# The sixteen remainders x_lo subtracted by GpSimd in VectorE's place

## What is computed

```
def _L0_cond_ref(x, thresholds, deltas, zero_points):       # G = 8 groups by |x|
    gi = jnp.sum(jnp.abs(x)[..., None] <= thresholds, axis=-1)
    idx = jnp.minimum(gi, G - 1)
    d = deltas[idx]; zp = zero_points[idx]
    x_quant = jnp.clip(jnp.round(x / d) + zp, 0, N_LEVELS - 1)
    return jnp.where(gi == G, jnp.float32(0), (x_quant - zp) * d)
...
x = x + _L0_ffn_ref(_L0_cond_ref(x, ...), router_w, A, B)    # top 2 of 4 low-rank experts
x = x + _L1_ffn_ref(_L1_cond_ref(x, itok, W, lora_A, lora_B_w), gate, kernel, bias, ...)
```

## Time and profile before

| | us |
|---|---|
| median of 3 runs | 467.94 (467.78 to 469.76) |
| profiled execution | 467.9 |
| its span | 466.1 |
| TensorE busy | 459.5 (99%) |
| VectorE busy | 389.0 (83%) |
| ScalarE busy | 356.8 (77%) |
| GpSimd busy | 5.4 (1%) |

### The profile page before, as it was taken

One profiled execution on the slowest core, in us unless ns is written; L12 is line 12 of the kernel. 1 busy time (PEld: TensorE's weight loads), 2 busy tenths in 40 slices (PEclk: granted clock), 3 DMA queues, 4 the chain that ended last, 5 costly groups with the idle time before them and its releaser, 6 DMA issues.

```text
span 466.1 us, 5628 instructions
## 1 busy us (share of the span) xinstructions
PE 459.5 (99%) x2182; PEld 353.3 (76%) x2182; DVE 389.0 (83%) x381; ACT 356.8 (77%) x299; POOL 5.4 (1%) x11
## 2 busy tenths in 40 slices
PE   8999999999999999999999999999999999999996
PEld 8537888888688887778777877787787778767874
DVE  1376989998999979999999999799899997999300
ACT  1499979893799799598599987995999797895001
POOL 0000000000000000000000000000000000000000
PEclk9999999999999999999999999999999999999999
DMA  8998324301244333505125107105214013011102
GB/s 273 363 368 334 99 57 148 101 12 51 61 127 167 92 49 101 191 1 157 43 104 157 58 1 234 69 4 158 91 56 159 0 56 136 28 30 45 46 1 90
DMA packets 35836, 50.35 MB, mean 108 GB/s; under 512 B 26626, under 2 KB 26882, under 8 KB 33538
## 3 DMA queue, kind: packets, MB, share of 16 engines
q1 hardware_dynamic: 34802, 42.66, 28.3%
q0 software_dynamic: 1008, 7.34, 4.2%
HBM read 39.51 MB, written 10.49 MB: 107 GB/s over the span
## 4 chain that ended last, share of the span: by engine, by line
PE 87%; ACT 4%; DMA 3%; DVE 2%; issue 2%; SPq 1%; ACTq 0%
PE bank L984 13%; PE bank L986 13%; PE bank L985 13%; PE bank L961 6%; PE bank L893 6%; PE bank L867 5%; PE bank L915 5%; PE bank L936 5%; PE bank L932 5%; PE bank L933 5%; DMA kst<-k_in 3%; PE bank L824 3%; PE bank L889 2%; PE bank L982 2%; ACT level L415 1%
## 5 line engine op out<-in xcount | busy, mean ns | idle before, releaser
L636 DVE COPY_PREDICATED val<-inside,val 128x2048 f32<-128x2048 uint8 x56 | 142.3, 2542 | 0.3
L426 ACT ACTIVATE val<-level,shift,small 128x2048 f32<-128x2048 int16 x64 | 133.9, 2091 | 2.3 <-PE bank L867 1.9
L415 ACT ACTIVATE level<-xq,inv 128x2048 int16<-128x2048 f32 x64 | 127.9, 1998 | 0.9
L984 PE MATMUL bank<-p_hi,x_hi 128*128 128x512 f32 x256 | 101.9, 398 | 0.0
L986 PE MATMUL bank<-p_hi,x_lo 128*128 128x512 f32 x256 | 100.1, 391 | 0.0
L985 PE MATMUL bank<-p_lo,x_hi 128*128 128x512 f32 x256 | 99.9, 390 | 0.0
L618 DVE TENSOR_SCALAR val<-val,width,unshift 128x2048 f32<-128x2048 f32 x64 | 86.0, 1344 | 9.5 <-ACT val L426 9.5
L627 DVE TENSOR_SCALAR inside<-absx,thr 128x2048 uint8<-128x2048 f32 x56 | 72.0, 1285 | 0.0
L984 PEld LDWEIGHTS bank<-p_hi,x_hi 128*128 128x128 f32 x256 | 48.1, 188 | 17.8 <-issue 9.2
L986 PEld LDWEIGHTS bank<-p_hi,x_lo 128*128 128x128 f32 x256 | 48.1, 188 | 10.5
L985 PEld LDWEIGHTS bank<-p_lo,x_hi 128*128 128x128 f32 x256 | 48.1, 188 | 10.1 <-issue 0.2
(11 more groups left out here) (91 smaller groups left out, 459.4 us busy)
## 6 DMA issues: line engine op xcount, KB each, us to landing
xs<-xt_in SPq DMA_DIRECT2D x8, 1024.0 KB, 4.9
out_t<-ost SPq DMA_DIRECT2D x16, 512.0 KB, 2.9
wst<-w_in SPq DMA_DIRECT2D x14, 512.0 KB, 3.7
xq<-xt_in POOLq DMA_DIRECT2D x7, 1024.0 KB, 5.5
la<-la_in SPq DMA_DIRECT2D x4, 512.0 KB, 5.3
lb<-lb_in SPq DMA_DIRECT2D x4, 512.0 KB, 12.4
kst<-k_in SPq DMA_DIRECT2D x4, 512.0 KB, 15.6
kst<-k_in SPq DMA_DIRECT2D x1, 2048.0 KB, 9.1
```

What stands on the lines that cost most here:

```text
L415: nc.scalar.activation(level[:, g % 2], xq[:, c % 2], ACT.Copy, scale=inv[:, group(g)]).then_inc(levels_made, 1)
L426: nc.scalar.activation(val[:, turn(c, g)], level[:, g % 2], ACT.Relu, bias=shift[:, group(g)], scale=par[:, 1, group(g)]).then_inc(raised, 1)
L636: nc.vector.copy_predicated(val[:, acc(c)], inside[:, g % 2], val[:, turn(c, g)]).then_inc(merged, 1)
L984: mm(o, x_hi[:, s, k, at], p_hi[:, h, k], start=False, stop=False)
```

## The change

The function `x_part` moves from VectorE's block to GpSimd's, and with it all sixteen subtractions. Each still waits for its half of x_hi (x_hi_made) and still counts x_lo_made, on which TensorE and the load of xs wait. The two for batch 0 stand on GpSimd at step 16, the others at j = 1 and 3. Between them the seven loads of xq keep their waits but get a place in the same order: `quant_input(c + 1)` stands where group 0 of batch c stands in GROUPS.

```diff
             # gpsimd
-            for c in range(1, BATCH):
-                quant_input(c)
+            def x_part(c, p):
+                pool.wait_ge(x_hi_made, c * XPARTS + p + 1)
+                part = slice(p * XK, (p + 1) * XK)
+                nc.gpsimd.tensor_tensor(x_lo[:, c % 2, part], xs[:, part], x_hi[:, c % 2, part].bitcast(F32),
+                                        ALU.subtract).then_inc(x_lo_made, 1)
+
+            quant_input(1)
+            for k in range(SLOTS):
+                for c, g in GROUPS[k]:
+                    if g == 0 and c + 1 < BATCH and c:
+                        quant_input(c + 1)
+                if k == STEPS:
+                    for p in range(XPARTS):
+                        x_part(0, p)
+                b, j = divmod(k - STEPS, KT)
+                if 0 <= b < BATCH - 1 and j in XAT:
+                    x_part(b + 1, XAT.index(j))
...
             # vector
             p_out(STEPS - 1)
-            for p in range(XPARTS):
-                x_part(0, p)
             dve.wait_ge(bias_hi_made, 1)
...
-                    if b + 1 < BATCH and j - 1 in XAT:
-                        x_part(b + 1, XAT.index(j - 1))
```

More of the change, by code:

```diff
@@ L730, in gate @@
                                         gates.unsqueeze(3).to_broadcast([P, TT, E, R0]), ALU.mult).then_inc(mg_made, 1)
[L732 to L736, removed]
             dve.wait_ge(ab_hi_made, 1)
```

## The result

The changed kernel takes 474.5 us (median of 4 executions, 471.35 to 479.36), the kernel before beside it 468.25 (4 executions, 467.78 to 469.76). The ratio is 1.010 (95% interval 1.007 to 1.014): slower by 1%, where 1.3% was forecast, with the median at almost the predicted time of 474.2. The profiled execution is the fastest of the four, 471.35, with a span of 469.6: 3.5 us over that of before. It shows half of what the median lost, and the other half had to be looked for.

A forecast was written before the change was run, and what follows sets the result against it. The prediction took TensorE, busy 459.5 of 466.1 us, as the bound, with VectorE almost a second. It added 4.2 at the last p_lo and 2.1 at batch 7's mid to 467.9, giving 474.2 us, range 467.2 to 481.

The forecast's parts named there:

- no hold: Rival: GpSimd doesn't hold VectorE, so p_lo comes when it came and the time is 467.9 to 467.4 us; chance 0.27.
- The 0.5 us that rows 7 allowed: TensorE's wait for VectorE's last p_lo, ending at 184.00; the most that any relief of VectorE can give.
- h = 2.2: Time in us for which each GpSimd subtraction makes VectorE stand still: two reads, 2.1, plus 0.12 for handing over.
- Heavier holds: Rival: each subtraction holds VectorE for 2.4 us or over, giving 476 to 481 us and more; chance 0.15.
- Term 1: At the last p_lo: batch 0's two subtractions go ahead of L723 and L726, making p_lo 4.2 us late.
- one hold: Rival at the last p_lo: only L726 waits, the second subtraction comes after it, 471.9 us; chance 0.12.
- Term 2: At the later mids: VectorE's lateness exceeds its margin only before the mid of batch 7, adding 2.1 us.
- The lateness r: How much VectorE is late against TensorE: 2.2 at batch 5, 3.8 at batch 6, 3.2 at batch 7.
- The two side sums: Totals for other hold lengths: 481.2 us at 2.7 us, and 475.6 us with the Trainium skill's figure.
- GpSimd isn't starved by a full stream: On GpSimd's access to the port: one load got in although VectorE's next instruction stood ready at 135.64.
- the place of the loads of xq: On GpSimd's queue: loads standing among or behind subtractions have a buffer's time in hand, costed at nothing.
- the reload of the library: On GpSimd's queue behind the third load: runs at about 136 us, 45 us before the first subtraction, costing nothing.

The follow-up runs named there:

- the exchange in the kernel before: Kernel before, no subtractions on GpSimd, with VectorE making the last p_lo ahead of the gates of batch 1: 467.8 us, ratio 0.9973.
- the copy with its one input: VectorE subtracts all sixteen as in the kernel before, each behind an added GpSimd copy of xs to x_lo: 470.18 us, ratio 1.004.
- the second trace: Profiled execution, 476.22 us, of the changed kernel measured once more with no edit: median 475.83 us, ratio 1.014.
- batch 0 alone: Changed kernel with only the two subtractions of batch 0 on GpSimd, the other fourteen back on VectorE: 475.25 us, ratio 1.010.
- The first trace: Profiled execution of the changed kernel in its first measurement, the fastest of four: 471.35 us.
- a late p_lo in the kernel before: Kernel before, with VectorE making batch 0's two x_lo and the bias remainder ahead of the last p_lo: 474.63 us, ratio 1.012.
- The doubled kernel: Changed kernel with each of the fourteen GpSimd subtractions of batches 1 to 7 made twice: 507.12 us, ratio 1.083.
- the kernel that waits for p_lo: Changed kernel with GpSimd also waiting for the last p_lo before its first pair of subtractions: 472.29 us, ratio 1.006.

## Why the prediction was right, and where it was not

**Direction and mechanism: right.** A subtraction on GpSimd stops VectorE, and this reaches TensorE at the two places named, the last p_lo and the mid of batch 7, and hardly at those of batches 5 and 6. The rival "no hold" is excluded by every 3.40 us TENSOR_SCALAR. The 0.5 us that rows 7 allowed came only from the exchange in the kernel before, and not from relief by GpSimd.

**h = 2.2: close, by a working that is not borne out.** Measured 2.02 to 2.14, mean of six held rows 2.08 (3.40 - 1.34, 3.40 - 1.36, 4.72 - 2.58, 4.65 - 2.58, 4.37 - 2.35, 3.42 - 1.28). "Heavier holds" is out as a matter of h. But the 2.2 was put together from two passes of 1.04 us, one for each input, and the copy with its one input held 0.8. That the sum of the two passes came so near is in part luck.

**Term 1, +4.2: right in size in two traces, with a rival true in the third.** 3.9 us in the second trace and in that of batch 0 alone. The first trace is the "one hold" case as that rival had it, with 1.7 us in place of 1.9: L738 (the old L723) ran free, only L741 was held, and the second subtraction came beside p_lo. The rival's 471.9 is near the 471.35 of that execution. So which of the two happens differs between two executions of the same kernel. For those without a trace it is argued from their times; their spread (469.8 to 480.4 for batch 0 alone) is that of the clock as well, with means from 1.00 down to 0.982.

**Term 2, +2.1: mis-sized, 1.3 measured.** The lateness r of VectorE ahead of batch 7 was to be 3.2. L718 of batch 6 starts at 398.00 without a wait, where L703 had waited 2.70 and started at 395.56; less TensorE's 2.35 that is r = 0.1, not 1.1. Two net holds of 2.08 - 1.13 = 0.95 make 2.0, and against the margin of 1.2 the wait is 0.8 (0.87 in the chain). Of that 1.0, 0.9 was gone by the last merge of batch 6: it ends at 388.62 + 4.65 = 393.27, 5.2 after that of before; less TensorE's 2.35 that is 2.9, where the prediction has 3.8. The four holds from batch 5 on put 8.24 us on VectorE (2.12, 2.02, 2.05 and 2.05), and the four subtractions that no longer stand there had taken 4.60 between the instructions around them: 3.64 in place of 4.28.

```profile
342.54 4.68 DVE L651 COPY_PREDICATED val<-inside,val 128x2048 f32<-128x2048 uint8 x1
...
348.48 4.37 DVE L657 SCALAR_TENSOR_TENSOR val<-absx,thr,val 128x2048 f32<-128x2048 f32 x1
```

TensorE's own lateness at batch 5 (0.14) and a merge that took 2.48 in place of 2.62 make up the rest. The remainder of the 1.3 is that mid itself is longer, 3.79 and 3.68 in place of 3.52, because its second half waits once more. In medians the fourteen later subtractions cost 0.8 us (469.39 and 468.62), in the profiled execution 1.5.

**Missing: the clock.** No term stands for what a TensorE wait of 4 us does behind itself. It was 1.5 us in the second trace, 2.3 with batch 0 alone, and 2.4 with a late p_lo in the kernel before. The sum that the runs support is 3.9 + 1.3 + 1.5 to 2.4 = 6.7 to 7.6 us on top of before; on the second occasion it was 7.2 (475.83 and 468.62). The first four executions have 6.3, and one of them at least had only one hold. So that the predicted 6.3 stands this close is luck in part: a term 0.8 too large stood beside one of about 2 that was absent. The doubled kernel came out 10 us above what I expected; some may lie in the base, as the expectation took the changed kernel at 471 to 475 and it has 475.83, and some in its mean clock of 0.959. The shares are not shown.

**Sums.** The two side sums of the prediction don't come out of its own steps. At h = 2.7 the lateness ahead of batch 5 is 3.9, and 3.9 + 2.7 - 2.2 gives 4.4 there in place of 3.5, so 482.1 us. At the h of 2.37 from the Trainium skill's figure the same steps give about 476.8 in place of 475.6. Neither bears on the forecast at 2.2.

**"GpSimd isn't starved by a full stream": right for the outcome, wrong in degree.** One load that got in between two instructions was too little to conclude from. In the first profile the subtractions took 2.4 to 7.9 us singly and up to 16.1 as a pair, in a stream nearly without gaps. It cost nothing since x_lo is wanted late, except where the start was put off (1.1 us at the first slot in the kernel that waits for p_lo). What decides at which boundary GpSimd gets in stays open.

**At nothing, and so it was:** the place of the loads of xq, and the reload of the library: no TensorE wait on either in any trace.

## What to carry to other kernels

Work moved from VectorE to GpSimd is not off VectorE if it reads SBUF: here, with two inputs, it stopped VectorE for 2.1 us to save 1.1. Look first at what small instruction stands ahead of the one that TensorE waits for, because a hold doesn't ask how long the held instruction is: eight elements cost as much as two thousand; putting the awaited one first gained a little in the kernel before, and took most of the loss out of the changed one (ratio 1.004 in place of 1.014). And price a wait of TensorE of about 4 us at its length plus what the lower clock takes, some 40% to 65% again here. Read the clock of every execution before laying a spread to the change: the kernel before has low-clock executions too.

## What the runs showed of the hardware that I had not expected

- At a TensorE wait of 4.1 to 4.4 us the granted clock fell to its lower level for a while in each of the four traces with such a wait, before its end or just behind it, at 1.5 to 2.4 us in the three where it was priced; behind one of 2.2 us it did not, and behind waits of 1.2 to 1.4 us at the mid of batch 7 it did in one trace and not in four. In 25 of 81 executions of the kernel before the mean clock is 0.996 or less, and no trace shows why.
- GpSimd can be passed over for 10.5 us (374.70 to 385.2) by a stream of VectorE's large instructions, and then gets in at two boundaries in a row.
- A fill on GpSimd leaves VectorE's merges and two-input instructions alone, waits itself beside TENSOR_SCALARs (0.95 to 3.38 us), and held three TENSOR_SCALARs by 0.47 to 0.78 us; a copy held instructions of every kind by 0.6 to 1.0 us, one by 0.4.
